# Layer 1 attention: another slot table for the projection pieces, and the output projection in eight half units

## The chip, the cores and the metric

The kernel runs on one core of a Trainium2 chip. The metric is the time of one execution on the device, in microseconds; the median of several executions is compared.

## The reference, cut to what matters

Two transformer layers run in one program over eight sequences of 512 tokens with 256 features: attention and a feed-forward part, twice. The change lies in the second attention ("L1 attention"):

```python
proj = x @ W_in.T + b_in                    # 256 -> 3 * 16 * 64
q, k, v = (16 heads of 64 columns each)
q = _rope(q, sin, cos); k = _rope(k, sin, cos)
att = softmax(where(causal, q @ k.T / 8, -inf))
y = att @ v                                 # per head, then the heads side by side
return y @ W_out.T + b_out                  # 1024 -> 256
```

x is layer-normalised before it and the result is added to x.

## The kernel before

`attention(block, 1, ...)` works through eight sequences, called batches here. A batch has 16 heads of three groups each, so 48 groups; group g of a head holds its query tiles (0, 1), (2) or (3). Time is laid out by hand in **slots**: slot k of a batch is one group, and k % 3 is the group's place g in its head. Each engine (TensorE is PE, VectorE is DVE, ScalarE is ACT, GpSimd is POOL) has its own instruction stream, which goes through the slots in order and, in each, through a fixed list. Batch 0 and batch 7 are written out, batches 1 to 6 are one hardware loop. What is left of a batch after slot 47 is done in the first slots of the next.

In slot k the engines do this, in this order:

- PE: scores of group k (L284, L285, L289), transposes of the probabilities of group k-2 (L298), probabilities times values of group k-4 (L318 to L320), then the **fills** of the slot into two PSUM work banks that take turns.
- ACT: `piece_hi` of a piece filled three slots ago (L484, L491, L493, L494), `hi` of group k-2 (L443), the taking of the slot's stack, xT and yT fills (L454, L459, L475), then `exp` of group k (L435).
- DVE: the output of a finished head (L548, L551), `lo` (L539), the taking of pieces and projections filled one slot ago (L580, L587, L601, L605), the row maximum of group k (L532), and `normalize` for the next batch (L611 to L621) in the slot before an xT fill.
- POOL: `piece_lo` of a piece filled four slots ago (L723, L727), then `rotate` of one filled in the slot before (L708, L710, L714).

Fills are:

- **stack**: q and k of the next head transposed, 8 transposes at k % 3 = 0 and 4 at k % 3 = 1 (L343).
- **piece**: 128 tokens times 512 columns of the input projection, six matmuls (L372). Each half of the heads needs 12 pieces: p = 0 to 7 are q and k pieces in turn (q even, k odd), p = 8 to 11 are v pieces. DVE takes a piece to `t_buf` (L580, a ring of four). For a q or k piece DVE multiplies by the cosines (L587, `rope_u`), POOL by the sines (L708, L710) and adds both (L714, `rope_z`, a ring of two); ACT waits for that before it copies the high part to the stage, and POOL subtracts it for the low part (L727). A v piece needs only ACT (L484) and POOL (L723).
- **xT**: transposes of a normalised tile of the next batch. **yT**: transposes of the outputs of two heads. **proj**: the output projection of one tile of 128 tokens over all eight chunks of yT (L389), added to x by DVE (L601), with new row statistics (L605).

The slot table is

```python
AT_1 = (1, 2, 4, 6, 8, 12, 14, 15, 16, 18, 19, 21)        # pieces of this batch, heads 8 to 15
AT_XT = (19, 20, 22, 23)
AT_0 = (24, 26, 28, 30, 33, 34, 36, 38, 39, 40, 42, 43)   # pieces of the next batch, heads 0 to 7
AT_PROJ, YT_LAG = (55, 56, 57, 58), 1                     # 55 is slot 7 of the next batch
```

`besides` adds work to batch 0 alone: POOL issues 28 indirect DMAs that add the results of the layer before to x (slots 0 to 3 and 20 to 43, L1318), DVE and ACT make statistics. ACT may not run ahead of POOL: in `piece_hi`

```python
wait(act, s_z, b * 16 + 8 * half + p + 1)     # rope_z of this piece
```

stands first in ACT's slot, ahead of `hi`, the stack and `exp` of that slot. PE needs `exp` of group k for the scores of group k+2, which write the same bank.

Of the kernel before, what the change touches and what calls it, by code (L numbers as in the profile page):

```python
# [52 lines left out]
LAGS = ((2, 2, 3, 4, 0, 1), (2, 2, 3, 4, 0, 1))  # L53


PE_ORDER = ("STFP", "STPF")

ACT_ORDER = ("HEW", "PHWE")

DVE_ORDER = ("OMNWL", "OLWMN")  # L60

# [51 lines left out]


def attention(block, layer, x_sb, stats, consts, w, sem, sb, banks, aside=None):

    LAG_T, LAG_HI, LAG_LO, LAG_PV, LAG_WA, LAG_WV = LAGS[layer]
    LAG_OUT = LAG_PV + 3
    L1 = layer == 1

    if L1:
        AT_1 = (1, 2, 4, 6, 8, 12, 14, 15, 16, 18, 19, 21)
        AT_XT = (19, 20, 22, 23)  # L130
        AT_0 = (24, 26, 28, 30, 33, 34, 36, 38, 39, 40, 42, 43)
        AT_PROJ, YT_LAG = (55, 56, 57, 58), 1
    else:
        AT_1, AT_XT, AT_0 = (4, 8, 11, 14), (20, 22, 25, 26), (29, 32, 35, 38)
        AT_PROJ, YT_LAG = (57, 58, 60, 61), 3
    DH = DH1 if L1 else DH0
    HC = P // DH
    CHUNKS = HEADS // HC
    FILLS = 2 if L1 else 1
    QW = 128 if L1 else K0  # L140
    KW = 192 if L1 else K0
    VW = 130 if L1 else 51
    OW = 65 if L1 else 51
    PIECES = 12 if L1 else 4
    S, PT, W, ob = banks[0:2], banks[2:5], banks[5:7], banks[7]
    LOW = F16 if L1 else BF16
    ident_f, ident_b, ident_h, mask = consts["ident_f"], consts["ident_b"], consts["ident_h"], consts["mask"]
    ident_l = ident_h if L1 else ident_b

    q_stage = sb(f"q_stage{layer}", [P, 2, QT, 8, QW], LOW)  # L150
    k_stage = sb(f"k_stage{layer}", [P, 2, QT, 8, KW], LOW)
    v_stage = sb(f"v_stage{layer}", [P, 2, QT, 8, VW], LOW)
    stack = sb(f"stack{layer}", [P, 2, (1 + FILLS) * T], LOW)
    xn = sb(f"xn{layer}", [P, 2, D], F32)
    xnT = sb(f"xnT{layer}", [P, 2, C, T] if L1 else [P, C, T], F16 if L1 else F32)
    prob = [sb(f"prob{layer}_{g}", [P, n], F32) for g, n in enumerate(GROUP_COLS)]
    p_hi = [sb(f"p_hi{layer}_{g}", [P, 2, n], F16) for g, n in enumerate(GROUP_COLS)]
    p_lo = [sb(f"p_lo{layer}_{g}", [P, 2, n], F16) for g, n in enumerate(GROUP_COLS)]
    one = sb(f"one{layer}", [P, 1], F32)
    neg_max = sb(f"neg_max{layer}", [P, QT], F32)  # L160
    y = sb(f"y{layer}", [P, 2, QT, P], F32)
    yT = sb(f"yT{layer}", [P, CHUNKS, T], F32)
    rsum = sb(f"rsum{layer}", [P, 2 if L1 else 1, QT * (1 if L1 else HC)], F32)
    if L1:
        t_buf = sb("t_buf", [P, 4, 512], F32)
        xn_part = sb("xn_part", [P, 2, 2, D], F16)
# [24 lines left out]
    s_dve = sem("bias_out_added")
    s_y = sem("y_ready")
    s_rs = sem("row_sums_inverted")
    s_xnT = sem("xnT_ready")
    s_yT = sem("yT_ready")
    s_proj = sem("x_updated")
    s_const = sem("stages_prepared")
    s_one = sem("one_ready")
    s_xs = sem("xn_step")
    s_u = sem("rope_cos_ready")  # L200
    s_z = sem("rope_ready")


    def work(k, last):

        out = []
        nxt = [] if last else [1]
        h, r = divmod(k, 3)
        if 0 <= k < GROUPS and r < FILLS:
            out += [("stack", 0, h + 1, r)] if h + 1 < HEADS else [("stack", 1, 0, r) for _ in nxt]  # L210
        out += [("piece", 0, 1, p) for p, at in enumerate(AT_1) if at == k]
        for _ in nxt:
            out += [("xT", 1, j) for j, at in enumerate(AT_XT) if at == k]
            out += [("piece", 1, 0, p) for p, at in enumerate(AT_0) if at == k]
        out += [("yT", 0, c) for c in range(CHUNKS) if k == 3 * (HC * (c + 1) - 1) + LAG_OUT + YT_LAG]
        out += [("proj", 0, i) for i, at in enumerate(AT_PROJ) if at == k]
        return out


    assert AT_PROJ[-1] - GROUPS < 3 * (HC - 1) + LAG_OUT + YT_LAG  # L220
    TAIL = AT_PROJ[-1] + 1 + LAG_WV
    FILLS_W = FILLS * HEADS + 2 * PIECES + QT + CHUNKS + QT
    assert FILLS_W % 2 == 0

    class Banks:


        def __init__(self):
            self.bank = 0
            self.t = Tally(FILLS_W - FILLS * HEADS)  # L230

        def next(self, kind):
            self.bank = 1 - self.bank
            if kind != "stack":
                self.t.add()
            return self.bank, self.t.value()

    def piece_parts(p):

        return (p % 2, p // 2) if p < 8 else (2, p - 8)  # L240

    def pieces(k, last):

        return [(ahead, *a) for kind, ahead, *a in work(k, last) if kind == "piece"]

    def run(eng, prologue, slot, tallies, next_batch=lambda: None, besides=None):

        def batch(b, first, last):
            next_batch()
            for k in range(GROUPS):  # L250
# [2144 lines left out]
```

## Time and profile before

| | us |
|---|---|
| median of 3 runs (2392.59 to 2395.78) | 2395.36 |
| the profiled execution | 2390.89 |
| its span, first to last instruction | 2389.1 |
| busy over the span: PE, DVE, ACT, POOL | 1989.0 (83%), 1752.3 (73%), 1469.8 (62%), 1032.4 (43%) |
| L1 attention, first xT fill to last statistics | 980.7 to 2077.7 |

In the profile an instruction's start is in us from the start of the span. PE's matmuls are pipelined, so the time that a group of them costs is read from its start to the start of the next group, not from its duration. A wait is put down to the instruction that ended it. The loop's batches repeat each other slot for slot.

### The profile page before, as it was taken

Reading aid. Unit: us, or ns where it says so; the run is one execution under the profiler, and the core shown is the slowest. Engines: PE = TensorE matmul, PEld = TensorE weight load, DVE = VectorE, ACT = ScalarE, POOL = GpSimd, SP = SyncE. Lnnn points to the kernel's source line nnn. Section 1 sums busy time; section 2 is a strip of 40 time slices with the busy share of each in tenths; the row PEclk is TensorE's granted clock in tenths of the full one; section 3 lists DMA queues with packets and bytes.
Section 4 is the critical chain, followed back from the end, with each engine's and each line's share of the span. In section 5 each row is a group of like instructions: output and inputs, shape, how many; then the busy total and the mean of one; then the engine's idle time right before and its main releaser. Section 6 shows DMA issues by size and latency. Waiting matters only on the chain. (4 is left out here: it accounts for less than half of the span.)

```text
span 2389.1 us, 57135 instructions
## 1 busy us (share of the span) xinstructions
PE 1989.0 (83%) x18502; PEld 1435.8 (60%) x18503; DVE 1752.3 (73%) x3653; ACT 1469.8 (62%) x2928; POOL 1032.4 (43%) x1226
## 2 busy tenths in 40 slices
PE   2989888898870999377799999989898999639999
PEld 1766666666660666145576667676666767525665
DVE  3877777787783444467678787969697887679997
ACT  1767666776661443266668686868687787434443
POOL 4425524354005000488746565647566574032222
PEclk8999999999955999699999999999999999859999
DMA  7000000000033323002100000000000000100000
GB/s 233 1 2 1 0 0 0 0 0 1 1 108 130 102 87 82 12 10 34 21 2 3 2 3 2 2 3 2 3 2 3 1 2 2 38 1 13 15 18 25
DMA packets 53114, 57.64 MB, mean 24 GB/s; under 512 B 7120, under 2 KB 47216, under 8 KB 52896
## 3 DMA queue, kind: packets, MB, share of 16 engines
q1 hardware_dynamic: 46240, 45.00, 6.1%
q0 software_dynamic: 6656, 9.85, 1.9%
q8 instruction: 122, 2.00, 0.4%
q14 instruction: 96, 0.79, 0.1%
HBM read 36.22 MB, written 18.61 MB: 23 GB/s over the span
## 5 line engine op out<-in xcount | busy, mean ns | idle before, releaser
L1033 ACT ACTIVATE prob_sb<-a_bank,neg_max_sb 128x128 f32<-128x128 f32 (+3 forms) x512 | 256.5, 530 | 164.6 <-DVE neg_max_sb L1113 153.3
L1113 DVE TENSOR_REDUCE neg_max_sb<-a_bank 128x1 f32<-128x128 f32 (+3 forms) x512 | 236.0, 483 | 119.0 <-PE a_bank L900 117.3
L372 PE MATMUL a_bank<-w_in_sb,xnT_sb 128*128 128x512 f16 x1152 | 290.2, 390 | 29.4 <-DVE t_buf_sb L580 20.7
L532 DVE TENSOR_REDUCE neg_max_sb<-a_bank 128x1 f32<-128x128 f32 (+3 forms) x512 | 235.1, 479 | 98.1 <-PE a_bank L289 97.3
L435 ACT ACTIVATE prob_sb<-a_bank,neg_max_sb 128x128 f32<-128x128 f32 (+3 forms) x512 | 259.3, 538 | 58.8 <-DVE neg_max_sb L532 54.5
L443 ACT ACTIVATE p_hi_sb<-a_bank 128x384 f16<-128x384 f32 (+1 forms) x384 | 204.5, 533 | 112.2 <-PE a_bank L298 111.1
L539 DVE TENSOR_TENSOR p_lo_sb<-a_bank,p_hi_sb 128x384 f16<-128x384 f32 (+1 forms) x384 | 227.1, 593 | 52.9 <-ACT p_hi_sb L443 50.6
L454 ACT ACTIVATE stack_sb<-a_bank 128x1024 f16<-128x1024 f16 (+1 forms) x256 | 209.8, 820 | 32.6 <-PE a_bank L343 30.9
L298 PE MATMUL a_bank<-ident_f_sb,prob_sb 128*128 128x128 f32 x1280 | 207.2, 277 | 0.6 <-ACT prob_sb L435 0.6
L913 PE MATMUL a_bank<-ident_f_sb,prob_sb 128*128 128x128 f32 x1280 | 205.6, 275 | 2.0 <-DVE probT_sb L1121 2.0
L708 POOL TENSOR_TENSOR rope_w_sb<-t_buf_sb,sin_sb 128x256 f32<-128x256 f32 x128 | 124.8, 975 | 169.8 <-DVE t_buf_sb L580 167.9
L318 PE MATMUL a_bank<-v_stage_sb,p_hi_sb 128*128 128x65 f16 x1280 | 159.4, 194 | 36.7 <-DVE y_sb L551 35.2
L372 PEld LDWEIGHTS a_bank<-w_in_sb,xnT_sb 128*128 128x128 f16 x1152 | 104.7, 100 | 137.8 <-DVE t_buf_sb L580 29.4
L284 PE MATMUL a_bank<-stack_sb 128*128 128x128 f16 (+3 forms) x512 | 149.3, 304 | 39.1 <-ACT prob_sb L435 29.1
L1216 POOL TENSOR_TENSOR parts_sb<-rest_sb,one_sb 128x256 bf16<-128x256 f32 x64 | 39.2, 612 | 310.6 <-DVE rest_sb L1138 310.6
L714 POOL TENSOR_TENSOR rope_z_sb<-rope_u_sb,rope_w_sb 128x512 f32<-128x512 f32 x128 | 162.8, 1272 | 23.9 <-POOL rope_w_sb L710 21.4
L580 DVE SCALAR_TENSOR_TENSOR t_buf_sb<-a_bank,bias_sb 128x512 f32<-128x512 f32 x192 | 131.3, 684 | 43.0 <-PE a_bank L372 30.4
L899 PE MATMUL a_bank<-stack_sb 102*128 102x128 bf16 (+3 forms) x512 | 143.0, 305 | 21.2 <-ACT prob_sb L1033 17.2
L319 PE MATMUL a_bank<-v_stage_sb,p_hi_sb 128*128 128x65 f16 x1280 | 160.2, 197 | 0.0
L320 PE MATMUL a_bank<-v_stage_sb,p_lo_sb 128*128 128x65 f16 x1280 | 158.3, 193 | 0.0
L285 PE MATMUL a_bank<-stack_sb 128*128 128x128 f16 (+3 forms) x512 | 155.4, 303 | 0.0
L913 PEld LDWEIGHTS a_bank<-ident_f_sb,prob_sb 128*128 128x128 f32 x1280 | 134.9, 142 | 29.9 <-DVE probT_sb L1121 5.3
(259 smaller groups left out, 5487.1 us busy)
## 6 DMA issues: line engine op xcount, KB each, us to landing
sorted_rows<-zeros_sb SPq DMA_DIRECT2D x1, 4992.0 KB, 22.0
x_in_sb<-sorted_rows SPq DMA_DIRECT2D x39, 128.0 KB, 2.1
sorted_results<-y_moe_sb SPq DMA_DIRECT2D x39, 128.0 KB, 1.7
x_sb_sb<-L_attn_x SPq DMA_DIRECT2D x8, 512.0 KB, 10.6
w_raw_sb<-L_ffn_gate_bank SPq DMA_DIRECT2D x8, 512.0 KB
w_raw_sb<-L_ffn_up_bank SPq DMA_DIRECT2D x8, 512.0 KB
w_raw_sb<-L_ffn_down_bank SPq DMA_DIRECT2D x8, 512.0 KB
out<-x_sb_sb SPq DMA_DIRECT2D x32, 128.0 KB, 1.7
```

What stands on the lines that cost most here:

```text
L298: last = pe.transpose(PT[g][:, n * P:(n + 1) * P], prob[g][:, n * P:(n + 1) * P], ident_f[:, :])
L319: pe.matmul(o, hi, v[:, 65:130], start=False, stop=False)
L372: last = pe.matmul(out, xnT[:, x, c, j * P:(j + 1) * P], w["in"][:, w_, c, cols], start=k == 0, stop=k == len(terms) - 1)
L435: last = act.activation(prob[g][:, off:off + L], S[(3 * h + g) % 2][:, off:off + L], ACT.Exp, bias=neg_max[:, i:i + 1])
L443: act.activation(p_hi[g][:, h % 2, :], PT[g][:, 0:GROUP_COLS[g]], ACT.Copy).then_inc(s_hi, 1)
L454: act.activation(dst, src, ACT.Copy).then_inc(s_stev, 1)
L532: last = dve.tensor_reduce(neg_max[:, i:i + 1], S[(3 * h + g) % 2][:, off:off + L], AX.X, ALU.max, negate=True)
L539: dve.tensor_tensor(p_lo[g][:, h % 2, :], PT[g][:, 0:GROUP_COLS[g]], p_hi[g][:, h % 2, :], ALU.subtract).then_inc(s_lo, 1)
L714: pool.tensor_tensor(rope_z[:, p % 2, :, :], rope_u[:, p % 2, :, :], rope_w[:, :, :], ALU.add).then_inc(s_z, 1)
L913: last = pe.transpose(PT[r][:, n * P:(n + 1) * P], prob[g][:, h % 2, off + kt * P:off + (kt + 1) * P], ident_f[:, :])
L1033: last = act.activation(prob[g][:, h % 2, off:off + L], S[(3 * h + g) % 2][:, off:off + L], ACT.Exp, bias=neg_max[:, i:i + 1])
L1113: last = dve.tensor_reduce(neg_max[:, i:i + 1], S[(3 * h + g) % 2][:, off:off + L], AX.X, ALU.max, negate=True)
```

## The change

`attention` (which served a first layer too) becomes `attention1`. Its code is the same but for the table, for the two halves of the output projection, and for the aside work of batch 0:

```diff
+LAGS1 = (2, 2, 3, 4, 0, 1)
+AT1 = ((1, 2, 4, 5, 7, 8, 10, 11, 13, 14, 16, 17), (17, 20, 23, 26),
+       (25, 26, 28, 29, 31, 32, 34, 35, 37, 38, 40, 41), (43, 44, 46, 47, 67, 68, 70, 71), 2)
+    AT_1, AT_XT, AT_0, AT_PROJ, YT_LAG = AT1
...
-        out += [("proj", 0, i) for i, at in enumerate(AT_PROJ) if at == k]
+        out += [("proj", 0, *divmod(n, QT)) for n, at in enumerate(AT_PROJ) if at == k]
...
-                i, = a
-                wait(pe, s_yT, (b + 1) * CHUNKS)
-                for c in range(CHUNKS):
+                part, i = a
+                chunks = range(part * CHUNKS // 2, (part + 1) * CHUNKS // 2)
+                wait(pe, s_yT, b * CHUNKS + chunks[-1] + 1)
+                for c in chunks:
                     last = pe.matmul(out[:, 0:D], yT[:, c, i * P:(i + 1) * P], w["out"][:, c, :],
-                                     start=c == 0, stop=c == CHUNKS - 1)
-                taken[bank] = (s_proj, QT, off, i + 1)
+                                     start=c == chunks[0], stop=c == chunks[-1])
+                taken[bank] = (s_proj, PROJ, off, part * QT + i + 1)
...
+                if part == 0:
+                    wait(dve, s_dve, tile + 1)
+                else:
+                    wait(dve, s_proj, b * PROJ + i + 1)
+                dve.tensor_tensor(x_tile, x_tile, W[bank][:, 0:D], ALU.add).then_inc(s_proj, 1)
+                if part == 1:
+                    wait(dve, s_proj, b * PROJ + QT + i + 1)
+                    dve.bn_stats(stats["bn"][:, bass.ds(tile, 1), :].rearrange("p o d -> p (o d)"), x_tile)
...
     def act_aside(act, k):
-        if k == 16:
+        if k == 13:
             roots(act, GROUP_B)
...
     def dve_aside(dve, k):
-        if k == 15:
+        if k == 12:
             partial_stats(dve, 1)
             variances(dve, GROUP_B)
-        if k == 17:
+        if k == 14:
             invert(dve, GROUP_B)
```

All pieces now stand at k % 3 = 1 or 2, one to a slot. Slots 67, 68, 70 and 71 are slots 19, 20, 22 and 23 of the next batch.

## Rows read from the trace of the kernel before

**Rows 1.** Stretches: from:to, length, busy time by engine, clock, DMA.
```profile
1433.61:1564.47 130.86, 118.81 (x1283) 89.58 (x1282) 103.36 (x208) 97.24 (x188) 77.10 (x72) 0.98 0.01 2
1508.39:1555.90 47.51, 45.45 (x526) 33.09 (x523) 41.99 (x84) 41.77 (x82) 37.29 (x35) 1.00 0.01 2
1033.05:1173.93 140.88, 111.52 (x1171) 78.35 (x1170) 109.08 (x254) 100.56 (x191) 119.82 (x101) 0.92 0.19 27
```
**Rows 2.** Timeline, DVE: first row maximum of batch 2 and of batch 7.
```profile
1303.13 0.62 DVE L532 TENSOR_REDUCE neg_max_sb<-a_bank 128x1 f32<-128x128 f32 x2 [2.49 <-PE a_bank L289]
...
1950.68 0.62 DVE L532 TENSOR_REDUCE neg_max_sb<-a_bank 128x1 f32<-128x128 f32 x2 [0.42 <-PE a_bank L289]
```
**Rows 3.** Timeline, PE, slots 34 to 37 of batch 3.
```profile
1532.15 0.38 PE L284 MATMUL a_bank<-stack_sb 128*128 128x512 f16 x1
...
1533.25 0.63 PE L383 MATMUL a_bank<-ident_f_sb,y_sb 128*128 128x128 f32 x4
1533.71 0.22 PE L284 MATMUL a_bank<-stack_sb 128*128 128x128 f16 x1
...
1534.86 0.39 PE L343 MATMUL a_bank<-ident_h_sb,q_stage_sb 128*128 128x128 f16 x4
...
1535.31 1.46 PE L372 MATMUL a_bank<-w_in_sb,xnT_sb 128*128 128x512 f16 x6
1536.60 0.33 PE L284 MATMUL a_bank<-stack_sb 128*128 128x384 f16 x1
...
1537.70 0.39 PE L343 MATMUL a_bank<-ident_h_sb,k_stage_sb 128*128 128x128 f16 x4
```
**Rows 4.** Timeline, PE: one output projection of batch 2, slot 9 of batch 3.
```profile
1464.97 3.72 PE L389 MATMUL a_bank<-w_out_sb,yT_sb 128*128 128x256 f32 x16
1468.52 0.33 PE L284 MATMUL a_bank<-stack_sb 128*128 128x384 f16 x1
```
**Rows 5.** Timeline, PE: waits in slot 4 of batch 3, and at the loop's end.
```profile
1445.34 0.19 PE L318 MATMUL a_bank<-v_stage_sb,p_hi_sb 128*128 128x65 f16 x1 [1.74 <-DVE y_sb L551]
...
1563.40 0.28 PE L284 MATMUL a_bank<-stack_sb 128*128 128x128 f16 x1 [3.07 <-issue]
```
**Rows 6.** The first stretch after a loop's end.
```profile
1564.00:1566.00 2.00, 2.00 (x19) 1.87 (x18) 1.09 (x3) 0.59 (x1) 0.00 (x0) 0.50 0.01 4
```
**Rows 7.** Timeline, POOL, slots 33 to 39 of batch 3: pieces 4, 5, 6.
```profile
1530.56 0.72 POOL L708 TENSOR_TENSOR rope_w_sb<-t_buf_sb,sin_sb 128x256 f32<-128x256 f32 x1 [0.41 <-DVE t_buf_sb L580]
1531.24 1.17 POOL L710 TENSOR_TENSOR rope_w_sb<-t_buf_sb,sin_sb 128x256 f32<-128x256 f32 x1
...
1537.16 1.16 POOL L727 TENSOR_TENSOR q_stage_sb<-rope_z_sb,q_stage_sb 128x512 f16<-128x512 f32 x1
...
1541.60 1.16 POOL L727 TENSOR_TENSOR k_stage_sb<-rope_z_sb,k_stage_sb 128x512 f16<-128x512 f32 x1
```
**Rows 8.** Timeline, POOL, ahead of batch 0: one piece's rotation.
```profile
994.82 0.72 POOL L708 TENSOR_TENSOR rope_w_sb<-t_buf_sb,sin_sb 128x256 f32<-128x256 f32 x1
...
996.29 1.26 POOL L714 TENSOR_TENSOR rope_z_sb<-rope_u_sb,rope_w_sb 128x512 f32<-128x512 f32 x1
```
**Rows 9.** Timeline, ACT, slot 37 of batch 3.
```profile
1538.07 0.66 ACT L493 ACTIVATE k_stage_sb<-rope_z_sb 128x512 f16<-128x512 f32 x1
...
1539.11 0.62 ACT L443 ACTIVATE p_hi_sb<-a_bank 128x512 f16<-128x512 f32 x1
```
**Rows 10.** Timeline, DVE: a q or k piece taken.
```profile
1532.82 0.67 DVE L580 SCALAR_TENSOR_TENSOR t_buf_sb<-a_bank,bias_sb 128x512 f32<-128x512 f32 x1
1533.62 0.84 DVE L587 TENSOR_TENSOR rope_u_sb<-t_buf_sb,cos_sb 128x512 f32<-128x512 f32 x1
```
**Rows 11.** Waits in batch 0 alone, 1033 to 1174: us, times, longest.
```profile
ACT k_stage_sb L493 <- POOL rope_z_sb L714: 12.9, 7, 4.2
```
**Rows 12.** Timeline, ACT, batch 7: one head without a piece.
```profile
2028.20 1.02 ACT L454 ACTIVATE stack_sb<-a_bank 128x1024 f16<-128x1024 f16 x1
...
2033.22 1.02 ACT L454 ACTIVATE stack_sb<-a_bank 128x1024 f16<-128x1024 f16 x1 [0.32 <-PE a_bank L343]
```

More of the change, by code:

```diff
@@ L52 @@
 AT0 = ((1, 4, 7, 10), (13, 16, 19, 22), (23, 24, 26, 27), (31, 34, 37, 40), 26, 29, (68, 73, 76, 77))
[L53 to L60, printed above, removed]
+LAGS1 = (2, 2, 3, 4, 0, 1)
+AT1 = ((1, 2, 4, 5, 7, 8, 10, 11, 13, 14, 16, 17), (17, 20, 23, 26), (25, 26, 28, 29, 31, 32, 34, 35, 37, 38, 40, 41), (43, 44, 46, 47, 67, 68, 70, 71), 2)
 LAG_PH, LAG_PL = 3, 4
@@ L1407, in l1_attention @@
     with nc.Block() as block:
-        attention(block, 1, x_sb, stats, consts,
+        attention1(block, x_sb, stats, consts,
                   {"in": w_in, "out": l1.w_out, "bias": bias, "bias_out": l1.bias_out, "cos": l1.cos, "sin": l1.sin},
```

1004 lines of the change are left out of this document (431 added, 573 removed).

## The prediction

> **What bounds the kernel now.** The stretches by time come first. A batch of the loop takes 129.5 us, from the first row maximum of batch 2 to that of batch 7 (647.55 us for five) [rows 2]. In batch 3 PE is busy 118.8 of 130.9 us, DVE 103.4, ACT 97.2, POOL 77.1 [rows 1]: PE leads, and none is full. In slots 24 to 43 it is nearly so: 45.5 of 47.5 us, while POOL, on the same eight q and k pieces, is busy 37.3 [rows 1]. The reader should keep that last number.
>
> Next the timeline of PE, for what each part costs when nothing holds it, start to start [rows 3]. A slot with k % 3 = 2 costs 1.10 (1532.15 to 1533.25), one with k % 3 = 0 with its eight stack transposes 1.60 (1533.71 to 1535.31), one with k % 3 = 1 costs 1.10 (1536.60 to 1537.70) and four transposes, 0.22 as half of the eight in 0.45. A head is 4.02. A yT is 0.46, a piece 1.29, an xT 0.22 (estimate, four transposes again), an output projection 3.55 [rows 4]. A batch is 16 x 4.02 + 24 x 1.29 + 8 x 0.46 + 4 x 0.22 + 4 x 3.55 = 114.1. The other 15.4 of 129.5 are gaps: 3.07 where PE waits for its next instructions at the loop's end [rows 5], about 1.5 for a slow clock behind it (granted 0.50, that is 1.2 of 2.4 GHz, in the 2 us shown after that idle stretch [rows 6]; 3 us of it is my estimate), and 10.8 of small waits, such as 1.74 for DVE in slot 4 [rows 5]. So an even table can win at most 10.8 per batch; the 4.6 stay.
>
> **Part by part.**
> *The split projection* removes nothing from PE: 4 x 8 chunks become 8 x 4, so 1.78 each. It adds four DVE additions per batch (0.4 each, estimate from L587's 0.84 for twice the elements [rows 10]), in slots 20 to 24 and 44 to 48 where DVE takes few pieces or none: nothing on the path. Were that cover gone, 1.6 per batch.
>
> *The pieces.* This is the step that decides. Eight q and k pieces now lie in slots 1 to 11 and 25 to 35, eleven slots each, where they lay in 1 to 15 and 24 to 38. What POOL does for one is read where it was never idle: it starts piece 4's rotation at 1530.56, follows with piece 5's, and begins its first low part at 1537.16, so two rotations take 6.65 with the 0.05 by which they overlap; from there low part plus rotation take 1541.60 - 1537.16 = 4.44 [rows 7]. In the new table the order on POOL is rotation, rotation, then six times low part and rotation. From the take of piece 0 to the last `rope_z`: 6.65 + 6 x 4.44 = 33.3 us.
>
> Now what PE has to do meanwhile. With piece 0 in slot s, ACT waits for piece 7's `rope_z` at the head of slot s + 13, with its `exp` behind it, and the scores of slot s + 15 wait for that. For s = 1, PE's slots 2 to 15 are 5 x 1.10 + 5 x 1.60 + 4 x 1.32 + 9 x 1.29 + 2 x 0.46 = 31.3 us. POOL's way from the same point is 1.3 (end of the fill, 1532.15, to the end of its take, 1533.49 [rows 3, 10]) + 33.3 + 2.3 on ACT: two k copies 1.04 [rows 9], then a high part and an `exp`, about 0.6 each by L443's 0.62. That is 36.9. Even with a proportional share of small waits (5%, as 45.5 in 47.5) PE would come to 32.9. POOL is the longer by 4, twice in a batch. Pieces 3 and 5 show it first; piece 7 is the latest.
>
> Behind ACT's wait are queued the high part, the stack or xT copy and `exp` of its slot; behind those, PE's scores two slots on; behind them DVE's row maximum. Batch 0 shows this now, as its POOL also issues DMAs (busy 119.8 of 140.9 [rows 1]): ACT waits for `rope_z` 7 times before a k piece alone, 12.9 us [rows 11].
>
> A batch of the loop after the change, point by point:
> - two stretches set by POOL, 2 x 36.9 = 73.8;
> - PE's slots 16 to 25: 4 x 1.32 + 3 x 1.10 + 3 x 1.60 = 13.4, pieces 3.9, xT 0.7, four half projections 7.1, yT 0.9: 25.9;
> - PE's slots 40 to 1 of the next batch, the same without xT: 25.3;
> - the loop's end, 4.6;
> - small waits in those 20 slots. By share of 10.8 they would be 4.5; I take 3.2, because `normalize` now stands in slots with k % 3 = 1, and not ahead of the head output for which PE waits.
>
> Sum 132.8, against 129.5: +3.3, six times +20.
>
> *A rule beside it.* In rows, POOL's two multiplies take 0.72 and 1.17 when DVE's L587 runs beside them [rows 7], and the whole rotation 2.73 (994.82 to 997.55) when it doesn't [rows 8]. That is the bound from below for POOL: low part 1.16 with rotation 2.73 is 3.9, and the way to the last `rope_z` 2 x 2.73 + 6 x 3.9 = 28.9 where I take 33.3. I take 33.3 because DVE issues L587 right behind every take, 0.80 later [rows 10], and POOL in a backlog is always at work then. The Trainium skill, "SBUF — State Buffer", section "SBUF: two separate sides", says that a GpSimd operation and a VectorE operation with two SBUF inputs take one shared port in turn, each for its whole instruction. By that rule the sum keeps the 33.3; without it, it would be the 28.9 of rival 1.
>
> *Statistics of batch 1* at slots 12 to 14 instead of 15 to 17: the same instructions, once, 11 slots after their last DMA is issued at slot 3. Zero; if the first xT at 17 came before them it would be a wait of a few us, but normalize at 16 is two slots behind.
>
> *Batch 0*: POOL is the bound, and its work (119.8) doesn't change; the first half gets a POOL stretch with one DMA issue more in it but has 2 pieces fewer behind it. +1, between -4 and +6.
> *Batch 7 and the end*: its first half had four whole projections and now has four halves, -7.1, and one POOL stretch, +3.3 with its ACT tail: -4. Heads 14 and 15 have no pieces; such a head takes 5.0 on ACT [rows 12], PE with two halves about 7.5: +5. The tail loses four halves, -7.1. Together -6.
>
> Total 20 + 1 - 6 = +15. Against the profiled execution's 2390.9 (span 2389.1 and 1.8 around it) that is 2406; the median shown is 4.5 higher, so 2395.4 + 15 = **2410**. Its own range is 2402 to 2420, by 2 us per batch either way in the small waits.
>
> **Rivals.**
> 1. *POOL doesn't bind, the even table wins.* For it: small waits of 10.8 are there to be had, and with 28.9 instead of 33.3 POOL's way is 1.3 + 28.9 + 2.3 = 32.5, under PE's 32.9. It decides from POOL's 29.3 or less for the eight pieces. Then a batch is 114.1 + 4.6 + about 6 = 124.7, -4.8, six times -29; with batch 7 at -9 and 0 for batch 0: 2357. Against it: the back-to-back pieces of rows 7 took 4.44.
> 2. *POOL binds, and the small waits vanish behind it*, since DVE and ACT catch up while PE stands: 132.8 - 3.2 = 129.6, no change in the loop, -5 outside: 2390.
> 3. *The stalls also cost clock.* PE idles in one piece of some us at the loop's end and its clock is halved behind [rows 5, 6]; batch 0, with such stalls, has mean clock 0.92 against 0.98 [rows 1]. If each of the 15 stretches does it once, 1.5 each: +22 on the forecast, 2432. Against it: 4 us are spread over three pieces.
>
> **How the numbers follow.** Forecast 0.45, rival 1 0.20, rival 2 0.20, rival 3 0.15. A change under 0.2% (4.8 us) is about what can't be told from none. Faster: rival 1 and half of rival 2, 0.30. Same: the rest of rival 2 and the forecast's low end, 0.15. Slower: 0.55. The range of 8 in 10 goes from 2384, the low side of rival 2, to 2432; it leaves out rival 1.
>
> **What would show it.** In the profile after: batches of about 133 us; ACT's waits for L714 in loop batches, now near none, several us each at the k pieces of slots 8, 11 and 14 and 32, 35 and 38; L714 to L714 at 4.44 without a gap; no slot above 5 us where slots 8 to 10 had whole projections; PE's 1.74 in slot 4 gone or hidden. A period of POOL near 3.9, or ACT not waiting for it, would make me wrong, and so would a take that comes later than 1.3 after its fill.

## The result and the profile after

The changed kernel takes 2436.85 us (median of 4 runs, 2434.83 to 2444.12) where the kernel before takes 2393.98 beside it (4 runs): ratio 1.0185, interval 1.0162 to 1.0209. It is slower by 42.9 us. The forecast was slower by 15, with a range that ended at 2432. The sign was right, the size was not.

Line numbers have moved: L951 is the row maximum (L532 before), L958 `lo`, L969 the head output (L551), L982 and L989 the take and `rope_u` (L580, L587), L1066, L1068 and L1072 POOL's rotation (L708, L710, L714), L1085 its low part (L727), L743 scores (L284), L772 probabilities times values (L318), L793 the stack (L343), L802 xT, L812 a piece, L819 yT, L826 the output projection (L389), L1001 its take.

The first row maxima of batch 2 and of batch 7 come first, on DVE's timeline of the kernel after, as in [rows 2]:

```profile
1322.47 0.62 DVE L951 TENSOR_REDUCE neg_max_sb<-a_bank 128x1 f32<-128x128 f32 x2 [3.80 <-PE a_bank L745]
...
2003.78 0.62 DVE L951 TENSOR_REDUCE neg_max_sb<-a_bank 128x1 f32<-128x128 f32 x2 [2.13 <-PE a_bank L745]
```

That is 681.3 for five batches, 136.3 each, against 129.5. From the first row maximum of batch 0 (1036.14) to that of batch 1 (1189.15) it is 153.0 against 140.9, batches 1 to 6 take 814.6 against 776.8, and from batch 7's to the last addition to x 125.6 against 126.6. So +12.1, +37.9 and -0.9. Ahead of these and behind them the profiled execution is 4.1 longer, in work that the change leaves as it was; it is also 7.3 above its median while that of before is 3.1 below its own, so the three terms are somewhat above what the medians (+42.9) hold.

Stretches of the kernel after, by engine and clock, as in [rows 1]: batch 0, batch 3, and in batch 3 PE's slots 2 to 15 and 26 to 39, from scores to scores:

```profile
1036.14:1189.14 153.00, 121.72 (x1195) 84.81 (x1194) 117.19 (x256) 102.69 (x191) 120.49 (x101) 0.89 0.18 25
1459.30:1595.91 136.61, 121.47 (x1283) 89.18 (x1281) 105.62 (x213) 97.91 (x188) 76.51 (x72) 0.98 0.01 2
1467.70:1505.78 38.08, 32.55 (x369) 22.82 (x366) 32.58 (x59) 28.52 (x54) 33.67 (x32) 1.00 0.01 2
1533.89:1572.82 38.93, 34.20 (x368) 23.46 (x367) 33.31 (x61) 29.07 (x56) 33.70 (x32) 0.96 0.01 2
```

No engine's total work explains 6.8 us a batch: PE has 2.7 more, POOL 0.6 less. In the two stretches PE, DVE and POOL are each busy 85 to 88% of the time.

POOL in the first of them, one piece in full on its timeline, and the last `rope_z`:

```profile
1477.27 0.72 POOL L1066 TENSOR_TENSOR rope_w_sb<-t_buf_sb,sin_sb 128x256 f32<-128x256 f32 x1 [1.24 <-DVE t_buf_sb L982]
...
1483.76 1.27 POOL L1072 TENSOR_TENSOR rope_z_sb<-rope_u_sb,rope_w_sb 128x512 f32<-128x512 f32 x1 [0.22 <-POOL rope_w_sb L1068]
1484.98 1.16 POOL L1085 TENSOR_TENSOR q_stage_sb<-rope_z_sb,q_stage_sb 128x512 f16<-128x512 f32 x1
1486.10 1.17 POOL L1066 TENSOR_TENSOR rope_w_sb<-t_buf_sb,sin_sb 128x256 f32<-128x256 f32 x1
1487.24 0.72 POOL L1068 TENSOR_TENSOR rope_w_sb<-t_buf_sb,sin_sb 128x256 f32<-128x256 f32 x1
1488.18 1.27 POOL L1072 TENSOR_TENSOR rope_z_sb<-rope_u_sb,rope_w_sb 128x512 f32<-128x512 f32 x1 [0.22 <-POOL rope_w_sb L1068]
1489.41 1.60 POOL L1085 TENSOR_TENSOR k_stage_sb<-rope_z_sb,k_stage_sb 128x512 f16<-128x512 f32 x1
...
1501.44 1.27 POOL L1072 TENSOR_TENSOR rope_z_sb<-rope_u_sb,rope_w_sb 128x512 f32<-128x512 f32 x1 [0.22 <-POOL rope_w_sb L1068]
```

From 1483.76 to 1488.18 is 4.42, and three more such steps reach 1501.44: the 4.44 of [rows 7], without a gap. The last one ends at 1502.71.

What PE and ACT wait for in batch 3 (us, times, longest; "issue" stands for nothing that the profile shows), of the kernel after:

```profile
PE a_bank L772 <- DVE y_sb L969: 10.0, 9, 2.0
PE a_bank L793 <- issue: 2.6, 1, 2.6
ACT k_stage_sb L916 <- POOL rope_z_sb L1072: 2.6, 5, 0.6
PE a_bank L743 <- issue: 1.4, 1, 1.4
```

and of the kernel before, in the same batch:

```profile
PE a_bank L318 <- DVE y_sb L551: 4.2, 4, 1.7
PE a_bank L284 <- issue: 3.1, 1, 3.1
```

The reader should see that POOL's full stream does not reach PE through ACT, as had been forecast: ACT waits 2.6 in all. PE's loss is booked on DVE's head outputs, 5.8 more than before. Why DVE is late for them shows on its own timeline, at the moment when POOL runs L1072 and L1085 above:

```profile
1487.68 0.68 DVE L982 SCALAR_TENSOR_TENSOR t_buf_sb<-a_bank,bias_sb 128x512 f32<-128x512 f32 x1
1488.48 1.52 DVE L989 TENSOR_TENSOR rope_u_sb<-t_buf_sb,cos_sb 128x512 f32<-128x512 f32 x1
...
1490.65 0.42 DVE L969 TENSOR_TENSOR y_sb<-a_bank,rsum_sb 128x256 f32<-128x256 f32 x1
```

L989 takes 1.52 there; it was 0.84 in [rows 10], and it is 0.69 at its shortest. The mean over the loop is 1.19, against 1.06 before: 16 times 0.13, so only 2.1 of DVE's work in a batch is new.

One thing more stands in the second stretch, on PE's timeline, slots 32 to 35:

```profile
1551.98 1.46 PE L812 MATMUL a_bank<-w_in_sb,xnT_sb 128*128 128x512 f16 x6
1553.28 0.22 PE L743 MATMUL a_bank<-stack_sb 128*128 128x128 f16 x1
...
1557.82 0.20 PE L772 MATMUL a_bank<-v_stage_sb,p_hi_sb 128*128 128x65 f16 x1 [1.97 <-DVE y_sb L969]
...
1558.34 2.74 PE L812 MATMUL a_bank<-w_in_sb,xnT_sb 128*128 128x512 f16 x6
1560.87 0.63 PE L743 MATMUL a_bank<-stack_sb 128*128 128x512 f16 x1
```

The same six matmuls take 1.30 to the next scores in slot 32 and 2.53 in slot 34. From 1558.35 on the granted clock is 0.50 (1.2 of 2.4 GHz) for 3.41 us, behind a wait of 1.97 for `y_sb`. It does this in slot 34 of all six loop batches; a wait of 1.8 for `y_sb` in the first stretch is followed by none. In the kernel before it falls in no stretch of the loop, only at the loop's end. This is the mechanism of rival 3.

### The profile page after: what moved, and what is told of

Read it like the earlier page. It is cut to its first block and busy times, and to the rows that moved or that the text cites. A ratio compares the mean times of both kernels' runs of the same rounds, so it can differ in the third digit from the quotient of the medians.

```text
span 2442.3 us, 57291 instructions
## 1 busy us (share of the span) xinstructions
PE 2017.5 (83%) x18502; PEld 1438.9 (59%) x18503; DVE 1780.2 (73%) x3685; ACT 1475.5 (60%) x2928; POOL 1030.1 (42%) x1226
## 5 line engine op out<-in xcount | busy, mean ns | idle before, releaser
L374 ACT ACTIVATE prob_sb<-a_bank,neg_max_sb 128x128 f32<-128x128 f32 (+3 forms) x512 | 256.4, 530 | 164.2 <-DVE neg_max_sb L454 153.0
L812 PE MATMUL a_bank<-w_in_sb,xnT_sb 128*128 128x512 f16 x1152 | 303.3, 404 | 18.0 <-DVE t_buf_sb L982 17.1
L958 DVE TENSOR_TENSOR p_lo_sb<-a_bank,p_hi_sb 128x384 f16<-128x384 f32 (+1 forms) x384 | 227.8, 595 | 92.4 <-ACT p_hi_sb L878 92.0
L951 DVE TENSOR_REDUCE neg_max_sb<-a_bank 128x1 f32<-128x128 f32 (+3 forms) x512 | 236.0, 481 | 72.7 <-PE a_bank L745 72.1
L772 PE MATMUL a_bank<-v_stage_sb,p_hi_sb 128*128 128x65 f16 x1280 | 159.0, 194 | 83.1 <-DVE y_sb L969 82.2
L1066 POOL TENSOR_TENSOR rope_w_sb<-t_buf_sb,sin_sb 128x256 f32<-128x256 f32 x128 | 120.1, 938 | 251.5 <-DVE t_buf_sb L982 249.4
L812 PEld LDWEIGHTS a_bank<-w_in_sb,xnT_sb 128*128 128x128 f16 x1152 | 106.4, 102 | 132.4 <-issue 26.4
L772 PEld LDWEIGHTS a_bank<-v_stage_sb,p_hi_sb 128*128 128x128 f16 x1280 | 121.1, 97 | 100.8 <-DVE y_sb L969 75.9
L989 DVE TENSOR_TENSOR rope_u_sb<-t_buf_sb,cos_sb 128x512 f32<-128x512 f32 x128 | 152.9, 1195 | 30.4 <-POOL rope_z_sb L1072 18.2
L1072 POOL TENSOR_TENSOR rope_z_sb<-rope_u_sb,rope_w_sb 128x512 f32<-128x512 f32 x128 | 163.7, 1279 | 24.0 <-POOL rope_w_sb L1068 21.4
L743 PE MATMUL a_bank<-stack_sb 128*128 128x128 f16 (+3 forms) x512 | 150.9, 308 | 18.8 <-issue 7.4
L982 DVE SCALAR_TENSOR_TENSOR t_buf_sb<-a_bank,bias_sb 128x512 f32<-128x512 f32 x192 | 131.1, 683 | 47.1 <-PE a_bank L812 33.6
```

What stands on the lines that cost most here:

```text
L374: last = act.activation(prob[g][:, h % 2, off:off + L], S[(3 * h + g) % 2][:, off:off + L], ACT.Exp, bias=neg_max[:, i:i + 1])
L772: pe.matmul(o, hi, v[:, 0:65], start=kt == 0, stop=False)
L812: last = pe.matmul(out, xnT[:, x, c, j * P:(j + 1) * P], w["in"][:, w_, c, cols], start=k == 0, stop=k == len(terms) - 1)
L951: last = dve.tensor_reduce(neg_max[:, i:i + 1], S[(3 * h + g) % 2][:, off:off + L], AX.X, ALU.max, negate=True)
L958: dve.tensor_tensor(p_lo[g][:, h % 2, :], PT[g][:, 0:GROUP_COLS[g]], p_hi[g][:, h % 2, :], ALU.subtract).then_inc(s_lo, 1)
L1072: pool.tensor_tensor(rope_z[:, p % 2, :, :], rope_u[:, p % 2, :, :], rope_w[:, :, :], ALU.add).then_inc(s_z, 1)
```

## The experiments

Each was compared with the kernel before in three rounds on one chip. "To before" is the ratio with its 95% interval. The slots' times are PE's, from the start of scores to the start of scores in batch 3. "Batch" is the mean from row maximum to row maximum over batches 2 to 6. Batch 3 is not always typical: the 38.8 of the short row maximum holds a fall of the clock like the one above, and the other five loop batches have 37.2 there. Where an edit below starts in the middle of a line, only the part of the table that differs is shown.

| kernel | median | to before | batch | slots 2 to 15 | 16 to 25 | 26 to 39 | 40 to 1 |
|---|---|---|---|---|---|---|---|
| before | 2393.98 | | 129.5 | 46.0 | 26.6 | 32.4 | 25.3 |
| after | 2436.85 | 1.0185 [1.0162, 1.0209] | 136.3 | 38.1 | 28.1 | 38.9 | 31.3 |
| pieces alone | 2438.54 | 1.0186 [1.0169, 1.0203] | 135.3 | 49.4 | 23.6 | 38.0 | 24.6 |
| split alone | 2417.19 | 1.0098 [1.0081, 1.0115] | 135.0 | 32.8 | 36.8 | 32.4 | 34.0 |
| short sines | 2394.97 | 1.0006 [0.9996, 1.0015] | 132.3 | 36.6 | 27.5 | 36.3 | 32.8 |
| short row maximum | 2414.4 | 1.0093 [1.0077, 1.011] | 133.2 | 38.8 | 26.7 | 37.5 | 32.0 |
| cosines from PSUM | 2402.55 | 1.0035 [1.0019, 1.0052] | 131.5 | 35.0 | 28.8 | 35.6 | 32.3 |
| both short | 2349.56 | 0.9811 [0.9793, 0.9829] | 125.9 | 34.8 | 26.8 | 32.7 | 32.8 |
| halves in POOL's stretches | 2456.78 | 1.0258 [1.0239, 1.0277] | 139.4 | 41.9 | 27.9 | 41.4 | 29.0 |
| old pieces, spread halves | 2379.84 | 0.9942 [0.9925, 0.996] | 128.1 | 43.1 | 28.0 | 32.4 | 25.2 |
| the same, new xT | 2413.47 | 1.0071 [1.0054, 1.0088] | 133.8 | 43.1 | 30.3 | 35.1 | 24.2 |
| the same, first halves early | 2401.79 | 1.0031 [1.0019, 1.0044] | 132.2 | 38.4 | 28.2 | 32.4 | 34.2 |
| after, old xT | 2461.27 | 1.028 [1.0263, 1.0297] | 140.4 | 38.1 | 31.9 | 38.1 | 31.4 |
| after, xT a slot later | 2465.15 | 1.03 [1.0282, 1.0317] | 140.5 | 38.1 | 30.2 | 41.6 | 31.1 |

### The pieces alone, and the split alone

The kernel before with only the new slots of the pieces:

```diff
-        AT_1 = (1, 2, 4, 6, 8, 12, 14, 15, 16, 18, 19, 21)
+        AT_1 = (1, 2, 4, 5, 7, 8, 10, 11, 13, 14, 16, 17)
-        AT_0 = (24, 26, 28, 30, 33, 34, 36, 38, 39, 40, 42, 43)
+        AT_0 = (25, 26, 28, 29, 31, 32, 34, 35, 37, 38, 40, 41)
```

> The kernel before with only AT_1 and AT_0 changed to the new ones; whole output projections stay at slots 7 to 10 of the next batch, xT and statistics where they were. Theory A (POOL sets the pace of the q and k stretches): slots 2 to 16 hold the same 8 pieces, but 14.2 us of projections as well, so PE (31.3 + 14.2 = 45.5) is the longer there and POOL hides behind it; slots 26 to 40 take about 37 us as in the changed kernel, against 32.6 before. A batch about +3, the kernel +15 to +25. Theory B (DVE, held at the port by POOL, sets the pace): the same for 26 to 40, and waits of PE for DVE's head output in 2 to 16 too; +25 to +40. If the split is what costs, this kernel is level with before.

The kernel after with only the split left, in its new slots; pieces, xT, the lag of yT and the statistics as before:

```diff
-AT1 = ((1, 2, 4, 5, 7, 8, 10, 11, 13, 14, 16, 17), (17, 20, 23, 26), (25, 26, 28, 29, 31, 32, 34, 35, 37, 38, 40, 41), (43, 44, 46, 47, 67, 68, 70, 71), 2)
+AT1 = ((1, 2, 4, 6, 8, 12, 14, 15, 16, 18, 19, 21), (19, 20, 22, 23), (24, 26, 28, 30, 33, 34, 36, 38, 39, 40, 42, 43), (43, 44, 46, 47, 67, 68, 70, 71), 1)
```

> The changed kernel with the old AT_1, AT_XT, AT_0, yT lag and statistics; the eight half projections stay at 43, 44, 46, 47, 67, 68, 70, 71. Both theories put the loss on the spacing of q and k pieces: slots 2 to 16 shrink by the 14.2 us of PE work that leave them (48.4 to about 35 to 37), slots 26 to 40 stay at 32.6, slots 16 to 26 and 40 to 50 grow by 7.1 each. A batch at 129 to 131: level with before within 8 us. If the halves at the loop's end cost more (wait for instructions 5.0 to 6.3 us there in the changed kernel), +1.3 a batch, +8 in all. If the split is what costs 40 us, it shows here.

Pieces alone: batch +5.8 and batch 0 148.3, which is +7.4; the kernel is 45 us slower, above both theories. Slots 2 to 15 now hold two pieces more than before and slots 26 to 39 one more, 1.29 of PE's time each. Less that, the first grow by 0.8 and the second by 4.3. So in the loop the new places cost where PE has no output projections to do meanwhile, as theory A says.

Split alone: batch +5.5 and batch 0 145.2, +4.4. So each part costs, and the split, in the places that the change gives it, costs 24 us where the forecast had nothing. In its loop batch the eight halves take 13.2 away from slots 2 to 15 and put 10.2 and 8.7 into 16 to 25 and 40 to 1, for 7.1 of PE work in each.

### POOL or DVE: which sets the stretches

The kernel after, with the multiplications by the sines on one head of the eight (the rest of `rope_w` is set to zero once, so seven heads lack their sine term):

```diff
-            pool.tensor_tensor(rope_w[:, :, 0:32], src[:, :, 32:64],
+            pool.tensor_tensor(rope_w[:, 0:1, 0:32], src[:, 0:1, 32:64],
...
-            own(pool.tensor_tensor(rope_w[:, :, 32:64], src[:, :, 0:32],
+            own(pool.tensor_tensor(rope_w[:, 0:1, 32:64], src[:, 0:1, 0:32],
...
+            pool.memset(rope_w[:, :, :], 0.0)
```

> The changed kernel; POOL's two multiplies by the sines work on one head of eight (the other seven heads lose their sine term), so about 0.5 us less each, 1.0 per piece, POOL's period 3.5 instead of 4.43. DVE's instructions are the same. Theory A: the two stretches fall from 38.2 and 37.4 to what PE needs, 32.9 to 34.5, a batch by 7 to 9 us, the kernel by 50 to 65 us against the changed one. Theory B: DVE's cosine multiply still meets POOL's longer operations (1.27 and 1.16) and the stretches fall by at most 2 us each, the kernel by 30 or less.

The kernel after, with row maxima over a quarter of the columns:

```diff
-  last = dve.tensor_reduce(neg_max[:, i:i + 1], S[(3 * h + g) % 2][:, off:off + L], AX.X, ALU.max, negate=True)
+  last = dve.tensor_reduce(neg_max[:, i:i + 1], S[(3 * h + g) % 2][:, off:off + L // 4], AX.X, ALU.max, negate=True)
```

> The changed kernel; the row maximum covers the first quarter of each tile's columns only, about 1.0 us less DVE work per head, none of it at the port that DVE shares with POOL. Theory A: POOL keeps its 4.43 per piece, so slots 2 to 16 and 26 to 40 stay within 1 us of 38.2 and 37.4; the rest may gain a little, the kernel 0 to 15 us. Theory B: PE's wait for the head output (10 us a batch) shrinks by 1.0 per head, the stretches by 4 us each, the kernel by 40 to 60 us.

Both edits together:

> The changed kernel with both cuts: POOL's sine multiplies on one head of eight (1 us less per piece; the sine term of seven heads is left out) and the row maximum over the first quarter of the columns (1 us less DVE work per head). The sines alone took the stretches from 38.2 and 37.4 to 36.4 and 34.6, the row maximum alone to 37.5 and 36.6. If POOL sets the pace and DVE is the next bound right under it, both together take them to PE's own 31.3 and 31.5 plus some waits, 32.5 to 34, and a batch to 125 to 128; if they act independently (sum of the single gains), 35.7 and 33.7.

The first stretch in the kernels with short sines and with both short (the columns of [rows 1]: PE, weight loads, DVE, ACT, POOL, clock):

```profile
1436.13:1472.76 36.63, 32.16 (x368) 22.73 (x365) 31.52 (x61) 28.35 (x54) 26.48 (x32) 1.00 0.01 2
```
```profile
1419.85:1454.69 34.84, 32.14 (x369) 22.73 (x365) 27.65 (x61) 28.05 (x54) 26.49 (x32) 1.00 0.01 2
```

POOL loses 7.2 of its 33.7, and the stretches shrink by 1.5 and 2.7 only, to 36.6 and 36.3; theory A of the short sines wanted 34.5 or less and fell. With DVE shorter instead, the stretches are 37.2 (without the fall of the clock) and 37.5, and the loop batch shrinks by 3.1. With both, the stretches fall to 34.8 and 32.7 (PE's own way was put at 32.9), the batch by 10.3, more than the 4.0 and 3.1 together. So two bounds lie close together, POOL's at 37.2 to 38.1 and one through DVE at about 36.4; removing one shows the other. What the second consists of is not shown. With the short sines DVE is busy for 31.5 of the 36.6, so it isn't full; and the row maximum stands between scores and `exp`, so its edit shortens that chain as well as DVE's work. In the kernel with the short row maximum, ACT's and PE's waits in a loop batch are these:

```profile
ACT k_stage_sb L916 <- POOL rope_z_sb L1072: 7.4, 6, 2.3
PE a_bank L772 <- DVE y_sb L969: 6.7, 8, 1.2
```

The wait that was forecast (ACT for `rope_z`, 7.4 in place of 2.6, longest 2.3) appears when DVE has less to do.

The last of this group leaves POOL's work and DVE's count of operations as they are, and takes the second SBUF input from `rope_u`: DVE multiplies the PSUM bank by 1/64 and the cosines, ahead of the take to `t_buf`. The bias is left out of the cosine term.

```diff
-    dve.tensor_tensor(rope_u[:, p % 2, :, :], t_buf[:, p % 4, :].rearrange("p (h d) -> p h d", d=64),
-                      w["cos"][:, t, j, :].unsqueeze(1).to_broadcast([P, 8, 64]), ALU.mult).then_inc(s_u, 1)
...
+    dve.scalar_tensor_tensor(out=rope_u[:, p % 2, :, :], in0=W[bank][:, :].rearrange("p (h d) -> p h d", d=64),
+                             scalar=1.0 / W1_SCALE,
+                             in1=w["cos"][:, t, j, :].unsqueeze(1).to_broadcast([P, 8, 64]),
+                             op0=ALU.mult, op1=ALU.mult).then_inc(s_u, 1)
```

> The changed kernel; DVE's multiply by the cosines reads the piece from the PSUM work bank (scaled by 1/64) instead of t_buf, ahead of the take, so it has one SBUF input and not two. It leaves out the input bias in the cosine term. If an operation with a PSUM input doesn't meet POOL at the port, it takes about 0.7 us always (now 0.7 to 1.6), POOL's 0.45 per piece goes too (period 4.0), and DVE needs no wait between its two operations. Theory A (POOL sets the pace): the stretches 38.2 and 37.4 fall by 8 x 0.45 = 3.5 each, a batch to about 129, the kernel by 40 to 50 us against the changed one. If the operations of DVE and POOL don't hold each other up but are slow for another reason: no change in POOL's period, the kernel by less than 10.

POOL's timeline of this kernel, over one piece, then DVE's in the same us:

```profile
1469.81 0.73 POOL L1066 TENSOR_TENSOR rope_w_sb<-t_buf_sb,sin_sb 128x256 f32<-128x256 f32 x1
1470.49 0.73 POOL L1068 TENSOR_TENSOR rope_w_sb<-t_buf_sb,sin_sb 128x256 f32<-128x256 f32 x1
1471.44 1.28 POOL L1072 TENSOR_TENSOR rope_z_sb<-rope_u_sb,rope_w_sb 128x512 f32<-128x512 f32 x1 [0.22 <-POOL rope_w_sb L1068]
1472.68 1.16 POOL L1085 TENSOR_TENSOR q_stage_sb<-rope_z_sb,q_stage_sb 128x512 f16<-128x512 f32 x1
1473.80 0.73 POOL L1066 TENSOR_TENSOR rope_w_sb<-t_buf_sb,sin_sb 128x256 f32<-128x256 f32 x1
```
```profile
1471.51 0.68 DVE L985 SCALAR_TENSOR_TENSOR rope_u_sb<-a_bank,cos_sb 128x512 f32<-128x512 f32 x1
```

`rope_u` (L985 here) takes 0.68 while L1072 runs beside it, where it took 1.52, and 0.685 in the mean. POOL's period is 3.99 in place of 4.43: neither of its multiplications is held up. Eight pieces at 0.44 less are 3.5; the stretches are 3.1 and 3.3 shorter, PE's wait for `y_sb` falls from 10.0 to 3.8 a batch, and the kernel gains 34 us on the changed one, short of the 40 to 50 expected. This confirms that 0.44 of POOL's time per piece is contention with `rope_u`. It does not tell which engine the stretches follow: the same edit takes 0.5 from each `rope_u` (1.19 to 0.685), some 4.0 of DVE's work in a stretch, and with POOL alone relieved by 7.2 they lost only 1.5 and 2.7.

The Trainium skill, "SBUF — State Buffer", section "SBUF: two separate sides", says that a GpSimd operation that reads SBUF and a VectorE operation with two SBUF inputs take a shared port in turn. The trace agrees in both directions: POOL's multiply takes 0.72 or 1.17, and DVE's `rope_u` 0.69 at its shortest, 0.84 in [rows 10] and 1.52 above.

### Where the halves stand

The kernel after with its halves in slots with k % 3 = 0 and no piece, six of them inside POOL's stretches, where PE has time:

```diff
-(43, 44, 46, 47, 67, 68, 70, 71), 2)
+(33, 36, 39, 42, 57, 60, 63, 66), 2)
```

> The changed kernel with the eight half projections at 33, 36, 39, 42, 57, 60, 63, 66, slots with k % 3 = 0 and no piece, five of them inside the two q and k stretches. Theory A: PE has 38.2 - 31.3 and 37.4 - 31.5, 6 to 7 us, to spare there, so slots 2 to 16 and 26 to 40 grow by 2 us each at most while 16 to 26 loses 5.3 of 29.5 and 40 to 50 loses 5.3 of 31.5: a batch at 127 to 130 against 136.3, the kernel 2355 to 2400. If PE were what fills those stretches, moving work into them gains nothing: a batch stays at 135 to 137.

It is slower, not faster, where the expectation was 127 to 130 a batch: 41.9 and 41.4 for the stretches. PE's timeline shows the new wait:

```profile
1516.08 2.52 PE L812 MATMUL a_bank<-w_in_sb,xnT_sb 128*128 128x512 f16 x6 [2.16 <-DVE x_sb_sb L1001]
```

A half in slot k holds a work bank until DVE takes it in slot k + 1, and a piece there wants the same bank in the same slot. In a batch PE waits 2.8 in two such places, and 2.9 where a half waits for ACT to take the stack from its bank.

The split alone, with the halves spread over slots near the four old ones:

```diff
-(43, 44, 46, 47, 67, 68, 70, 71), 1)
+(51, 53, 55, 57, 58, 59, 61, 65), 1)
```

> The old tables for pieces, xT, yT and statistics, with the eight half projections at 51, 53, 55, 57, 58, 59, 61, 65, slots of the next batch without a piece. Before, four whole ones lay in slots 7 to 10 with 5.4 us of gaps in slots 2 to 16; eight halves have eight gaps to fall into. Expected a batch at 126 to 129 against 129.5 before, the kernel 0 to 20 us under before. If a half next to few pieces costs its full 1.8 to 1.9 us and fills no gap, level with before.

2379.84: 0.6% faster than the kernel before, and the fastest of those that leave no work out. So halves that are spread gain 1.4 a batch, and what cost 5.5 was their place. Whether the gain needs the halves is not shown, since four whole projections spread the same way were not run. A further kernel asks which part of the place costs. In it only the first four halves move, from the far side of the loop's end to this side:

```diff
-(51, 53, 55, 57, 58, 59, 61, 65), 1)
+(43, 44, 46, 47, 58, 59, 61, 65), 1)
```

> The kernel with the old pieces and spread halves (2379.8), with only its first four halves moved to slots 43, 44, 46 and 47, across from the far side of the loop's end. Theory A, that what the split costs in its place is bank and DVE waits in the crowded slots 67 to 71 (19 to 23, where pieces and xT lie): the loop batch grows by no more than 1, 2380 to 2386. Theory B, that work put ahead of the loop's end makes PE wait there a second time for its instructions: slots 46 to 2 grow by about 2 more than the work moved, 2392 or so, with two waits of more than 1 us for instructions each time round. The old pieces with all halves in the new slots took 2417.2.

Theory B's 2392 lay nearer than A's 2380 to 2386, and still short: 2401.8, batch +4.1. Slots 40 to 1 grow by 9.0 for 7.1 of work, and slots 2 to 15 give back only 4.7 of it. PE's timeline at the loop's end has two waits that the profile books on "issue". They stand where the loop jumps back, so I take them for waits for instructions; no row shows what they wait for:

```profile
1571.51 0.23 PE L743 MATMUL a_bank<-stack_sb 128*128 128x128 f16 x1 [1.82 <-issue]
...
1574.28 0.26 PE L745 MATMUL a_bank<-mask_sb,ident_b_sb 128*128 128x128 bf16 x1 [2.21 <-issue]
```

4.03 together, against one of 2.66 with the halves spread. That is 1.4 of the 4.1; another 2.4 is what slots 2 to 15 don't give back, where the four halves had cost 4.7 and not 7.1. The clock also stands at 0.50 for 6.83 us there in each pass, against 3.41 in two of five passes with the halves spread; what that costs is not divided from the rest.

### The xT fills and the statistics

The kernel with old pieces and spread halves, with xT and statistics as in the change:

```diff
-(19, 20, 22, 23), (24, 26,
+(17, 20, 23, 26), (24, 26,
...
-        if k == 16:
+        if k == 13:
             roots(act, GROUP_B)
```

> The kernel with the old pieces and spread halves (2379.8), with one part of the change more: xT fills at 17, 20, 23 and 26 and the statistics of batch 1 at slots 12 to 14. The forecast costed both at nothing: 2380, within 3. Rival: the xT in slot 26 meets the q piece of that slot, and the xT in slot 17 the slack that DVE needs for normalize; then up to 2 us per batch, 2392. The move of the statistics alone can cost at most what DVE and ACT do there once, some 3 us.

The rival held, at three times its bound of 2 us: batch +5.8. In batch 0 slots 0 to 15, where the statistics now lie, don't change (34.3 from slot 2 to 16 by row maxima in both); slots 16 to 25 grow from 27.3 to 34.2. So the statistics are free, and xT is not. DVE's timeline in slot 16 of batch 3:

```profile
1497.97 0.55 DVE L951 TENSOR_REDUCE neg_max_sb<-a_bank 128x1 f32<-128x384 f32 x1
1498.44 0.41 DVE L1010 TENSOR_SCALAR xn_sb<-x_sb_sb,mv_sb,rstd_sb 128x256 f32 x1
...
1500.07 1.37 DVE L1018 TENSOR_TENSOR x_sb_sb<-x_sb_sb,bias_out_sb 128x256 f32 x1
1501.37 0.68 DVE L958 TENSOR_TENSOR p_lo_sb<-a_bank,p_hi_sb 128x512 f16<-128x512 f32 x1
```

`normalize` holds DVE for 2.9 between the row maximum of one slot and the takes of the next, and PE shows what queues behind it:

```profile
1500.10 0.40 PE L802 MATMUL a_bank<-ident_h_sb,xn_part_sb 128*128 128x128 f16 x4 [1.03 <-DVE xn_part_sb L1016]
1502.70 0.66 PE L819 MATMUL a_bank<-ident_f_sb,y_sb 128*128 128x128 f32 x4 [2.21 <-DVE t_buf_sb L982]
```

The same question in the changed kernel, with xT back at its old slots:

```diff
-(17, 20, 23, 26), (25, 26,
+(19, 20, 22, 23), (25, 26,
```

> The changed kernel (2436.9) with its xT fills back in slots 19, 20, 22 and 23. In the kernel with the old pieces and spread halves the new xT slots cost 5.4 to 5.8 us a batch, mostly where PE waits for DVE's normalize, 1.03 to 1.3 at each of three xT, and for the take of the piece queued behind it. If that price is the same here, the batch shrinks by 4 to 5: 2405 to 2412. Rival: here slots 17 to 26 hold four half projections as well, and the old xT slots put an xT, a half and a yT into slots 20 and 23 with two work banks, as in the kernel with the split alone, whose slots 16 to 26 took 34.9 against 29.5 here: then no gain, or up to 5 us a batch of loss, 2437 to 2470.

And with xT one slot later:

```diff
-(17, 20, 23, 26), (25, 26,
+(18, 21, 24, 27), (25, 26,
```

> The changed kernel (2436.9) with its xT fills a slot later, at 18, 21, 24 and 27, so that each normalize stands in a slot with k % 3 = 2 and each xT in one with k % 3 = 0, away from the half projections and the yT. If the price is in the place of normalize, between the row maximum of one slot and the takes and head outputs of the next, the batch shrinks by 2 to 4: 2415 to 2427. Rival: normalize in the slot before a head output delays that output, for which PE waits in the slot after; then no gain, 2433 to 2445.

The first theory fell in both: 2461 and 2465, 4 us a batch slower than the changed kernel. The rival held for the old slots; for the later ones the result lies above its 2433 to 2445 too. With halves in 19, 20, 22 and 23, an xT there as well makes stack, xT and half three fills of slots 19 and 22 in two work banks. PE's timeline of the kernel with the old slots has the wait for ACT's taking of the stack, in slot 19:

```profile
1518.11 1.99 PE L826 MATMUL a_bank<-w_out_sb,yT_sb 128*128 128x256 f32 x8 [0.94 <-ACT stack_sb L888]
```

That kind of wait is 1.4 in slots 16 to 25, which grow by 3.8; waits for `y_sb` are 2.2 more there. With the later slots the xT itself waits, 3.3 in slots 16 to 25 and 2.5 in 26 to 39, behind DVE's taking of a half or of a piece from the bank. In the table of the change the new xT slots are worth 4.1 a batch. The kernel with the old ones also gives the sum of the parts: pieces +5.8, split +5.5, together 11.3, and it measures +10.8 (140.4 - 129.5). The new xT takes 4.1 back, and +6.8 is left.

## Why the prediction was right and wrong

**Bottom-up sum of a loop batch.** Forecast 132.8, measured 136.4 by PE's slots. Term by term in batch 3:

| | forecast | measured |
|---|---|---|
| slots 2 to 15 | 36.9 | 38.1 |
| slots 26 to 39 | 36.9 | 38.9 |
| slots 16 to 25 and 40 to 1, with the loop's end and small waits | 59.0 | 59.4 |

The failed step in the loop is the pair of POOL stretches, put at 36.9 each and measured at 38.1 and 38.9: 3.2 of the 3.6, times six some 19 us. POOL's period stood: 4.42, no gap from the fourth piece on in the first stretch. The size was off. In the first stretch `rope_z` of piece 7 is done 34.7 after the take of piece 0 (1467.99 to 1502.71), not 33.3, of which 1.24 is POOL's wait for the third take; PE was itself 1.7 late for it, waiting for `y_sb` in slot 4. In the second stretch the clock falls as well; where it doesn't, in the kernel with the old xT slots, the same slots take 38.0 to 38.1. And the sum let POOL stand alone: no way through DVE was given a bound. The short sines put one at 36.3 to 36.6, right beneath POOL's and above the 32.9 that the forecast had for PE. With the shorter row maximum the stretches come down to 37.2 and 37.5, near the 36.9. DVE's 41.99 of 47.51 in [rows 1], for eight pieces as well, was there to be read, and I didn't carry it to the shorter stretch.

**How the stall reaches PE** was wrong. I expected ACT's waits of several us for `rope_z`; they are 2.6 a batch, none above 0.6. PE waits 10.0 for `y_sb` instead: `rope_u` is held up to 1.52, DVE falls behind with head outputs, and PE waits for those. With the cosines from PSUM both go together, the held `rope_u` and 6.2 of the 10.0. How much of the 10.0 is due to POOL's backlog alone is not shown: `rope_u` was held before too (1.06 in the mean, against 1.19), and DVE now has the same eight pieces in a shorter stretch.

**"Nothing on the path" for the split, and nothing for xT,** failed taken singly (+5.5; -4.1 in this table and +5.8 in another), though their sum with the small waits came out within 0.4. That agreement is luck: two errors with opposite signs, and the 3.2 of small waits was a share and not a reading.

**Batch 0**: forecast +1, measured +12.1. An omission first: its own first four halves now lie in its slots 43 to 47, where batch 1 used to do them. The split alone shows +4.4 for that. The rest is the pieces, +7.4 when moved alone: I had POOL's total work as the bound, and that doesn't change (119.8 and 120.5). But PE's wait for `y_sb` goes from 9.1 to 18.5 in it: a sum over the whole batch hides what a stretch inside it costs.

**Batch 7 and the end**: -6 forecast, -0.9 measured. By row maxima slots 2 to 25 shrink by 3.7 (forecast 4) and slots 26 to 47 grow by 5.3 (5). Slots 0 and 1 grow by 1.4, which had no term, and the tail gives 3.9 and not 7.1.

**Rivals.** Rival 1 needed POOL at 29.3 for eight pieces; it stayed at 34.7. Even with POOL cut to 26.5 of work in a stretch, the kernel is at 2395, not 2357. Rival 2 let the small waits vanish; they didn't.

Rival 3 (stalls that cost clock) came nearest with its time, and its mechanism is there in part. The clock falls in one of the two stretches of every loop batch, not in both; the mean of batch 3, 0.98 as before, hides it. Its price is less than the 1.5 each that the rival took. Slots 26 to 39 take 38.7 to 38.9 in the six batches of the changed kernel, all with a fall; with the old xT slots they take 38.0 to 38.1 in five batches without and 38.6 in one with. So by estimate at most 0.9 a batch, 5 us of the 42.9.

In batch 0 the mean clock is 0.89 against 0.92. The first stretch there (slots 2 to 15, the same work in all three kernels, by row maxima) takes 42.3 in the changed kernel with 10.24 us at 0.50, and 40.8 both with the old xT slots and with the halves in POOL's stretches, with 3.41 us at 0.50. So 1.5 of batch 0's growth goes with the clock; for the rest of the batch no run tells.

**What stays open.** What the bound through DVE consists of, its work or the chain from scores to `exp`, is not known. The new waits at the loop's end explain 1.4 of the 4.1 that the early first halves cost, and the slots that they left 2.4; what the longer fall of the clock adds is not divided. Of batch 0's +7.4 for the pieces alone only the place (slots 2 to 15 and 26 to 39) is known: with short sines the whole of batch 0 comes to 138.6, so POOL's pace has a part in it.

## What to carry to other kernels

Sum the work of every engine in the stretch that is to be compressed, not of the fullest alone. Here three engines at 85 to 88% held each other up before any one was full, and an experiment that relieved one showed only the distance to the next. If two engines contend, as POOL and DVE do here, look for the price also at those who wait for the other one. Look at the clock stretch by stretch, since a mean over a batch hid a fall in each one. In a table of slots, price what is moved with what already stands there: the same xT move cost 5.8 us a batch in one table and was worth 4.1 in another, and the one part worth keeping, smaller units of output projection, gained 0.6% when spread near their old place and lost 1% in two clusters.

## What was not expected of the hardware

At the end of the hardware loop PE has its waits booked on "issue", once for 3.07 before [rows 5]. In every kernel with halves in slots 33 to 47 it waits twice, some 3 us apart: 1.36 and 2.29 after, 1.65 and 2.66 with the split alone, 1.82 and 2.21 with the first halves early, 2.78 and 1.94 with the halves in POOL's stretches. With none there it waits once, 2.66 with the halves spread and 2.54 with the pieces alone. These are the passes from batch 3 to batch 4; the other passes of each kernel show the same number of waits where they are above 0.9. PE's timeline of the kernel after:

```profile
1595.26 0.23 PE L743 MATMUL a_bank<-stack_sb 128*128 128x128 f16 x1 [1.36 <-issue]
...
1598.33 0.22 PE L793 MATMUL a_bank<-ident_h_sb,q_stage_sb 128*128 128x128 f16 x1 [2.29 <-issue]
```

What decides between one and two was not tried.
